# TensorE's filler products between a state-space scan and a mixture of experts: with them and without

## The reference, cut to what matters

```python
x = x + L0_conv(gn(x))        # in_proj, 3x3 conv, four selective scans, y * silu(z), out_proj
t = tokens(x)                 # 512 tokens of 64 channels
t = t + L1_attn(ln(t))        # q, k, v; each token sees 3 neighbours on either side; softmax
t = t + L1_ffn(ln(t))         # router over 8 experts, the best 2; silu(h1) * h3, hidden size 682
```

```python
y = y * silu(z); y = y @ out_proj_w
Q = x @ Wq.T + bq; K = x @ Wk.T + bk; V = x @ Wv.T + bv
scores = einsum('bnd,bnwd->bnw', Q, Kw) / scale
probs  = softmax(scores); out = einsum('bnw,bnwd->bnd', probs, Vw)
logits = flat @ router_w.T
h = silu(h1) * h3; y = einsum('neh,ech->nec', h, w2)
```

## Time and profile before

| | |
|---|---|
| time, median of 3 runs | 250.86 us (250.72 to 251.13) |
| time of the profiled execution | 253.52 us |
| its span in the trace | 251.8 us |
| PE busy (matmul) | 222.2 us, 88% |
| DVE busy | 179.3 us, 71% |
| ACT busy | 137.8 us, 55% |
| POOL busy | 139.1 us, 55% |
| mean granted clock | 0.964 |

### The profile page before, as it was taken

How to read it: one execution, slowest core, us unless ns; L and a number is a source line. 1 busy time by engine, 2 the same in 40 slices (tenths; PEclk the granted TensorE clock), 3 DMA queues, 4 the chain that set the end, 5 groups by cost and what they waited for, 6 DMA issues and landing times. The chain is left out here.

```text
span 251.8 us, 2856 instructions
## 1 busy us (share of the span) xinstructions
PE 222.2 (88%) x738; PEld 96.3 (38%) x738; DVE 179.3 (71%) x280; ACT 137.8 (55%) x204; POOL 139.1 (55%) x135
## 2 busy tenths in 40 slices
PE   7989849999789987998776999993999999999992
PEld 2323213423234232423222255662444555554530
DVE  4504997999999999999999654368654463544642
ACT  4136995967768876896657323453232433444430
POOL 5620999777998789977999900008007608400000
PEclk9999986999999999999999998999599999999999
DMA  5699300000000000000000900000900200100000
GB/s 152 140 209 207 55 0 1 3 1 0 0 0 0 0 0 0 3 0 1 1 0 9 215 0 3 0 0 0 211 14 0 56 0 16 42 0 0 0 0 21
DMA packets 8004, 8.56 MB, mean 34 GB/s; under 512 B 6646, under 2 KB 7223, under 8 KB 7480
## 3 DMA queue, kind: packets, MB, share of 16 engines
q1 hardware_dynamic: 7992, 8.42, 15.4%
HBM read 8.29 MB, written 0.13 MB: 33 GB/s over the span
## 5 line engine op out<-in xcount | busy, mean ns | idle before, releaser
L404 POOL TENSOR_TENSOR rings<-rings 128x512 f32<-128x512 f32 x64 | 80.1, 1271 | 12.4 <-DVE rings L652 12.1
L879 PE MATMUL ps<-rings,ident 128*128 128x512 f32 x128 | 70.7, 634 | 12.7 <-POOL rings L404 12.2
L652 DVE TENSOR_TENSOR_SCAN rings<-rings,ps 128x512 f32<-128x512 f32 x64 | 76.0, 1208 | 0.2 <-ACT rings L502 0.2
L807 DVE TENSOR_TENSOR gl<-ps,si 128x512 f32<-128x512 f32 (+1 forms) x44 | 30.4, 691 | 35.5 <-ACT si L565 35.4
L565 ACT ACTIVATE si<-ps 128x512 f32<-128x512 f32 (+1 forms) x44 | 26.2, 597 | 46.7 <-PE ps L1014 42.4
L502 ACT ACTIVATE rings<-delta,a_neg 128x510 f32<-128x510 f32 x64 | 44.1, 712 | 3.3 <-DVE rings L652 3.0
L510 ACT ACTIVATE rings<-ps 128x1024 f32<-128x1024 f32 x32 | 32.6, 1018 | 22.9 <-POOL rings L404 22.9
L645 DVE TENSOR_TENSOR ps<-ps,du 128x512 f32<-128x512 f32 x64 | 42.4, 686 | 2.0 <-PE ps L891 1.8
L879 PEld LDWEIGHTS ps<-rings,ident 128*128 128x128 f32 x128 | 22.0, 193 | 40.4 <-POOL rings L404 36.3
L421 POOL TENSOR_TENSOR wup<-wraw,wup 64x2728 fp32r<-64x2728 f32 x3 | 18.1, 6026 | 25.0 <-issue 24.8
L1014 PE MATMUL ps<-fh,wup 128*128 128x512 f32 (+1 forms) x88 | 31.3, 437 | 0.7 <-DVE gl L807 0.7
(11 more groups left out here) (172 smaller groups left out, 187.9 us busy)
## 6 DMA issues: line engine op xcount, KB each, us to landing
wraw<-w_up_dram SPq DMA_DIRECT2D x8, 682.0 KB, 7.2
wdn<-w_down_dram SPq DMA_DIRECT2D x4, 160.0 KB
w_conv<-conv_w_dram SPq DMA_DIRECT2D x1, 576.0 KB, 4.4
wdn<-w_down_dram SPq DMA_DIRECT2D x4, 128.0 KB
xg<-x_grp_dram SPq DMA_DIRECT2D x1, 128.0 KB, 2.7
xc<-x_chan_dram SPq DMA_DIRECT2D x1, 128.0 KB, 3.0
xt<-x_tok_dram SPq DMA_DIRECT2D x1, 128.0 KB, 2.0
out_dram<-res SPq DMA_DIRECT2D x1, 128.0 KB, 1.7
```

The source lines that it names most:

```text
L404: nc.gpsimd.tensor_tensor(hc[:, q], hs[:, q], cs[:, q], ALU.mult).then_inc(weighted, 1)
L652: nc.vector.tensor_tensor_scan(hs[:, q, :], da[:, q].rearrange("p b l -> p (b l)"), driven(q), 0.0, ALU.mult, ALU.add).then_inc(scanned, 1)
L807: nc.vector.tensor_tensor(gl[0:rows, S % 4, :], ps[0:rows, BANK_H + 2 * (S % 3) + 1, :], si[0:rows, S % 2, :], ALU.mult).then_inc(glu_read ...
L879: nc.tensor.matmul(ps[:, BANK_Y, :], ident[:], hc[:, q % BODY, :], start=False, stop=last_state).then_inc(y_ready if last_state else summe ...
```

## The change

All calls of `keep_warm` behind the last sum are left out: 3, 12, 2, 8, 16 and 4 products, 45 in all. The waits, the products that compute something, and the other engines' programs stay as they are, and so do the fillers at the start and in the scan.

```diff
             for n in range(K * N - LAG, K * N):
                 sum_state(n, n)
-            keep_warm(3)
             pe.wait_ge(out_in, 16)
             for t in range(NT):
                 pe.wait_ge(yg_ready, t // 2 + 1)
...
             last.then_inc(op_ready, 1)
-            keep_warm(12)
             for t in range(NT):
                 pe.wait_ge(tn_ready, t // 2 + 1)
...
                     last.then_inc(tnT_ready, 1)
-            keep_warm(2)
             pe.wait_ge(tnT_kept, 3)
             pe.wait_ge(qkv_in, 32)
...
             pe.wait_ge(v_kept, 1)
-            keep_warm(8)
             for t in range(NT):
                 pe.wait_ge(pr_ready, t + 1)
...
             last.then_inc(o_ready, 1)
-            keep_warm(16)
             for t in range(NT):
                 pe.wait_ge(tn_ready, B + t // 2 + 1)
...
             last.then_inc(fT_ready, 1)
-            keep_warm(4)
             pe.wait_ge(fT_kept, 1)
```

## The result

The change makes the kernel slower. The median went from 251.0 to 260.06 us, a ratio of 1.033 (95% interval 1.024 to 1.042); the four executions with the change lie between 256.65 and 260.49. Ratios are taken over the fast executions alone, so they can differ a little from the ratio of two medians. The direction was forecast. The size, 254.9 us, was not, and both medians with the change lie outside the range of 252.4 to 257.6.

A forecast was written before the change was run, and what follows sets the result against it. It took the stage for a chain of latencies across DVE, ACT and TensorE's small products, then unbroken expert products. Filler gains, low-clock costs and -1.1 behind the stall summed to +4.0 us: 254.9 us on the median, range 252.4 to 257.6.

The forecast's parts named there:

- Output projection: Eight products behind the last sum: without the 3 fillers before them they end earlier, gain 0.2 us.
- L953: Eight transposes: +0.9 us if all run at the low clock, 0 if the clock falls behind them; taken as +0.4.
- L961: Four 512-column f32 products for q and k: spacing doubles from 0.43 us at the low clock, +1.7 us.
- Probabilities to L987's end: Last probabilities through products with v: 4.35 us at low clock against 4.1, turning 1.6 us of gain into +0.2.
- Router and first tile: L1001's eight products +0.7 us and the first expert tile's four L1014 +0.7 at low clock, together +1.4.
- weight loads don't slow down: Rival: loads at L963, L987, L1001 take 0.11 us at either clock; sum +0.8, time 251.6 us, chance 0.09.
- Behind the stall: Expert products after TensorE's stall: one short low stretch instead of 5.9 us, -1.1 us, bounds 0 and -2.8.
- I keep 254.9: Whole kernel: +4.0 us set on the median of 250.86, not on the profiled 253.52, which gives 257.5.
- My first effect: Products behind too long filler runs start earlier; mainly the 8 before the softmax's transposes, 1.6 us; high-clock sum -1.9 us.
- Longer low stretch behind the stall: Rival: expert tiles stay low 6 us or more behind the stall; 0 to +2, 256 to 258 us, chance 0.12.
- Faster because the fillers were in the way: Rival: 8 fillers before the transposes give 1.6 us, other runs 0.3; time 248.9 us, chance 0.05.
- The clock's fall: TensorE's clock falls somewhere from 149 to 152 us and stays low through the attention.

The follow-up runs named there:

- e11: The kernel with the change, unchanged, one more execution: 259.38 us.
- e12: The kernel before, unchanged, one more execution: 250.83 us.
- e1: The kernel before, unchanged, timed again against itself over 12 executions: 251.22 us, ratio 1.0007.
- e2: The kernel with the change, unchanged, timed again against the kernel before with more executions: 258.56 us, ratio 1.0293.
- e3: Kernel before with only the 8 fillers in front of the transposes of the probabilities left out: 255.21 us, ratio 1.013.
- e7: Kernel before with all 45 fillers behind the scan kept, but 16 columns wide instead of 512: 258.55 us, ratio 1.028.
- e4: Kernel before, all fillers kept, GpSimd's first subtraction waiting for the first layer norm instead of the first expert tile: 246.14 us, ratio 0.979.
- e6: Kernel before with only the first three runs of fillers (3, 12 and 2) left out: 257.46 us, ratio 1.024.

## Why the prediction was wrong in size

**The sum itself, against the execution that it was made from.** I had +4.0 us; the traces of before and after show 4.1 behind the sum. The profile has every sign that I named for it: q and k in 3.68 us, v and the router at doubled spacing, L978's products (now L970) right behind the probabilities, L754 ending with L421 and longer, L421 5.3 us later behind the sum, and a shorter low stretch behind the stall. By terms:
- Output projection: -0.2 forecast, 0 measured. The eight products start 0.6 us behind the sum with and without fillers: they follow DVE's first half, and the second half is there in time.
- L953: +0.4 forecast, as a mean of 0 and 0.9; 0 in four executions, +0.9 in one (e11).
- L961 +1.7, measured 1.75. L963 +0.9, measured 0.9. The scores' first half +0.4, measured 0.5.
- Probabilities to L987's end: +0.2 forecast. Against the first trace 0.3, but against e12 1.9. See below.
- L995 +0.25, measured 0.4. Router and first tile +1.4, measured 1.6. The weight loads of the router's products take 330 ns at the low clock and 188 at the high one, so the rival "weight loads don't slow down" fell. With it falls, for this form, what the Trainium skill, TensorE: Matmul & The Clock Gate, section "LDWEIGHTS (loading the stationary operand)", would give by columns alone.
- L754 held until L421's end: right in both, 0.05 us behind it.
- Behind the stall: -1.1 forecast; -1.2 against the first trace, 0 against e12.

That the total fits within 0.1 us is partly luck: the output projection, L953 and the router's term were each off by 0.2 to 0.4 us, in both directions.

**The step that failed** is the base: "I keep 254.9", the sum from one execution set on the median of others. I had written that the profiled run lay 2.7 us over the median, that its low stretch at 155 might be the cause, and that the change would then cost up to 1.2 us more; then I gave it no weight. The runs showed in its place that the first trace of before held two pieces that an execution near the median need not have. The eight fillers at the low clock held the chain by 1.6 us; they are nearly all of the difference between 106.0 and 104.2 (e1). The low stretch behind the stall was nearly twice as long as in e12, which is the 1.1 us between 104.2 and 103.1. Together that is 2.9 us, and just these two were counted as what the change gives back. (I had written "8 x 0.2 = up to 1.2 us" for the first; the product is 1.6. The fillers themselves took 1.2 us longer, and the scores in front of them 0.5.) Against e12, which took 250.83 us and so is like the median, the change costs 6.9 us, all of it in front of the stall's end. On the median that gives 257.8. The range failed with the base: its own bounds, added up straight, reach 257.7 for the likeliest case, and I wrote 256.6.

**What is left** to 258.56 (e2) and 260.06 (first comparison) is 0.8 and 2.3 us. L681 starts between 145.8 and 147.9 us in the five traces of the kernel with the change, and between 146.4 and 147.0 in e3 to e7, which have other filler sets or another wait and the same scan. The three traces of before have 145.6 to 146.0, near the early end. So the scatter is in the scan, where no instruction changed; the scan of e4, which keeps all 45 fillers, ends late too (146.85). From this I argue that it doesn't belong to the change. It is not shown: only profiled executions have a timeline, and in none of its three did the kernel before end its scan late.

**My first effect was misread.** I took 1.6 us as the price of a run that is too long. It is the price of that run at the low clock. I had forecast 2.5 us from the last probability to the end of the products with v, without fillers and at the high clock; e1 takes 2.45 with the fillers in. So at the high clock the eight delay nothing, and there is no gain to set against the loss. e3 agrees: taking the eight out alone costs 3.3 us.

**The rivals.** Longer low stretch behind the stall: in all five traces it was short, about 3.3 us (184.1 to 187.4 us in the first), so no. Weight loads: no. Faster because the fillers were in the way: no. The clock's fall (forecast from 149 to 152) came between 150.5 and 153.6; it was low at q and k in all five.

## What to carry to other kernels

Products without a use can be worth 3%, if between two dense stages lies a chain of small products that TensorE can't fill: it is the low clock of the real products behind the gaps that costs (here 3.68 us instead of 1.93 for q and k). Such runs can't be judged one by one: a run sized for the high clock gets in the way once the clock is low, so leaving out the first 17 of 45 cost 5.9 of 7.4 us. And before a sum is set on a median, read the low stretches of the profiled execution: those that the change would touch must be priced with and without.

## What the runs showed of the hardware

- A weight load of 128 columns in f32 slows with TensorE's clock: the router's take 188 ns at the high level (before) and 330 ns at the low one (after). Its products move only 8 columns each, and the eight take 1.06 and 1.87 us.
- Products of 65 rows by 64 columns with 512 columns to stream, back to back at the low clock for 3.68 us, stood at the low clock in all five traces, and the clock stayed low behind them. In e6 it was high again behind eight fillers of 128 by 128.
- A DVE operation of 0.19 us took up to 4.43 us beside one GpSimd operation. Letting GpSimd's operation start at the first layer norm instead of at the first expert tile (e4) was worth 2.1%, 4.9 us.
